# A four-layer graph network: one hand-written order of steps for every engine replaced by another, with a table of banks

## What is computed

```python
def _L0_gnn_ref(x, adj, Wq, bq, Wk, bk, Wv, bv, Wo, bo, gamma, beta):
    ...
    logits = jnp.einsum('bhqd,bhkd->bhqk', q, k) / np.sqrt(DK)
    logits = logits + jnp.log(jnp.clip(adj, ADJ_MIN, None))[:, None, :, :]
    attn = jax.nn.softmax(logits, axis=-1)
    out = jnp.einsum('bhqk,bhkd->bhqd', attn, v)
    out = out.transpose(0, 2, 1, 3).reshape(b, n, d)
    out = out @ Wo.T + bo
    return _layer_norm(x + out, gamma, beta)

def _L1_gnn_ref(feats, adj_mat, fc_w, fc_b, q_w, q_b, k_w, k_b):
    ...
    feat_proj = jnp.einsum('bnh,oh->bno', feats, fc_w) + fc_b
    q = jnp.einsum('bnh,oh->bno', feat_proj, q_w) + q_b
    k = jnp.einsum('bnh,oh->bno', feat_proj, k_w) + k_b
    logits = q + jnp.swapaxes(k, 2, 1)
    masked = logits + (1.0 - adj_mat) * NEG_INF
    masked = jnp.where(masked >= 0, masked, LEAKY_SLOPE * masked)
    atten = jax.nn.softmax(masked, axis=-1)
    out = jnp.einsum('bnm,bmh->bnh', atten, feat_proj)
    return out + feats

def _L2_gnn_ref(x, adjacency, W_q, b_q, W_k, b_k, W_v, b_v, w_g, b_g):
    ...
    scores = jnp.einsum('bihd,bjhd->bhij', Q, K) / jnp.sqrt(jnp.float32(hd))
    soul_bias = a[:, :, None] + c[:, None, :] + b_g
    scores = scores + (soul_bias + jnp.log(adjacency + EPS))[:, None, :, :]
    attn = jax.nn.softmax(scores, axis=-1)
    out = jnp.einsum('bhij,bjhd->bihd', attn, V).reshape(B, N, D)
    return out + x

x = _L0_gnn_ref(x, adj, ...)
x = _L1_gnn_ref(x, adj, ...)
x = _L2_gnn_ref(x, adj, ...)
x = _L3_gnn_ref(x, adj, ...)   # as _L1, with other weights
return x
```

## Time and profile before

| | us |
|---|---|
| median of 3 runs | 1798.22 |
| lowest and highest | 1797.73, 1798.81 |
| span of the profiled execution | 1798.2 |
| PE busy | 1757.7 |
| DVE busy | 1475.6 |
| ACT busy | 1372.0 |
| POOL busy | 731.3 |

### The profile page before, as it was taken

The page is one execution under the profiler, slowest core; times in us unless marked ns, Lnnn a source line. Parts: engine busy times, 40 slices in busy tenths (PEclk is TensorE's granted clock), DMA queues, the critical chain, the costliest instruction groups (busy, mean ns, idle before and its releaser), DMA issues.

```text
span 1798.2 us, 68824 instructions
## 1 busy us (share of the span) xinstructions
PE 1757.7 (98%) x28155; PEld 1647.2 (92%) x28155; DVE 1475.6 (82%) x3361; ACT 1372.0 (76%) x3792; POOL 731.3 (41%) x797
## 2 busy tenths in 40 slices
PE   7999999999999999999999999999999999999997
PEld 6899999999999999999999999999999999999986
DVE  4688888888888888888888888888888888888875
ACT  3677787777787787787787787787787787787774
POOL 3343344343443343443443343343443443443421
PEclk8999999999999999999999999999999999999999
DMA  3101011011011011011011011011011011011100
GB/s 116 39 20 49 26 49 49 26 49 50 26 49 49 26 49 49 27 49 49 26 49 50 26 49 50 26 49 49 26 49 49 26 49 49 26 49 49 35 8 25
DMA packets 48261, 74.56 MB, mean 41 GB/s; under 512 B 5456, under 2 KB 21968, under 8 KB 47952
## 3 DMA queue, kind: packets, MB, share of 16 engines
q1 hardware_dynamic: 47376, 69.49, 12.1%
q10 hardware_dynamic: 576, 0.68, 0.1%
HBM read 53.37 MB, written 16.78 MB: 39 GB/s over the span
## 4 chain that ended last, share of the span: by engine, by line
PE 87%; ACT 3%; DMA 3%; DVE 3%; issue 2%; POOL 2%; SPq 0%; DVEq 0%; POOLq 0%; ACTq 0%
PE banks L1111 15%; PE banks L1176 14%; PE banks L1113 13%; PE banks L1112 13%; PE banks L1325 7%; PE banks L1220 6%; PE banks L1211 6%; DMA x_t<-x_t_dram 3%; PE banks L1199 2%; PE banks L1285 2%; PE banks L1225 2%; PE banks L1313 1%; PE banks L1319 1%; POOL weights_B L684 1%; PE banks L1279 1%
## 5 line engine op out<-in xcount | busy, mean ns | idle before, releaser
L684 POOL TENSOR_TENSOR weights_B<-weights_B,adj 128x512 f32<-128x512 f32 x64 | 113.0, 1766 | 299.1 <-ACT weights_B L765 299.1
L690 POOL TENSOR_TENSOR inv_parts_A<-inv_both_A,own 128x512 fp32r<-128x512 f32 x64 | 66.7, 1042 | 303.7 <-DVE inv_both_A L1035 303.7
L1000 DVE TENSOR_REDUCE least_cols_A<-banks 128x4 f32<-128x512 f32 x256 | 159.4, 684 | 33.8 <-PE banks L1176 33.7
L1000 DVE TENSOR_REDUCE least_B<-banks 128x4 f32<-128x512 f32 x256 | 172.6, 681 | 11.6 <-PE banks L1185 11.5
L1111 PE MATMUL banks<-w_hi_v,xt_hi 128*128 128x258 f32 (+1 forms) x512 | 157.3, 307 | 9.5 <-DVE pick L883 9.5
L1111 PE MATMUL banks<-w_hi_f,xt_hi 128*128 128x258 f32 x512 | 162.3, 317 | 2.3 <-DVE xt_lo L875 0.7
L839 ACT ACTIVATE fp<-banks 128x258 f32<-128x258 f32 x256 | 92.6, 390 | 89.1 <-PE banks L1113 89.1
L765 ACT ACTIVATE banks<-banks,v_B 128x256 f32<-128x256 f32 x384 | 153.4, 474 | 0.0
L1111 PE MATMUL banks<-xt_hi,w_hi_k 128*128 128x256 f32 x512 | 150.7, 294 | 0.3 <-DVE xt_lo L875 0.3
L1113 PE MATMUL banks<-w_lo_v,xt_hi 128*128 128x258 f32 (+1 forms) x512 | 145.1, 283 | 0.0
L1112 PE MATMUL banks<-w_hi_v,xt_lo 128*128 128x258 f32 (+1 forms) x512 | 145.0, 283 | 0.0
(11 more groups left out here) (192 smaller groups left out, 6172.0 us busy)
## 6 DMA issues: line engine op xcount, KB each, us to landing
x_t<-x_t_dram SPq DMA_DIRECT2D x64, 256.0 KB, 3.6
x_in<-x_dram SPq DMA_DIRECT2D x64, 256.0 KB, 3.6
out_dram<-x_out SPq DMA_DIRECT2D x64, 256.0 KB, 2.4
adj_t<-adj_t_dram SPq DMA_DIRECT2D x64, 128.0 KB, 3.4
adj<-adj_dram SPq DMA_DIRECT2D x64, 128.0 KB, 2.0
scratch<-weights_dram SPq DMA_DIRECT2D x9, 256.0 KB, 6.6
...
```

Of the source, the lines that this page charges most:

```text
L684: pool.tensor_tensor(units, units, weight_of[where][:, G.four, :, :].unsqueeze(2).broadcast_to([P, GROUP, 2, P]), ALU.mult).then_inc(first ...
L1000: dve.tensor_reduce(to, bank[SCORE_BANKS[n]].rearrange("p (u m) -> p u m", u=UNITS), axis=AX.X, op=ALU.min).then_inc(maxed[where], 1)
```

## The change

The operations are the same. Every engine gets a new order of the steps of a turn (ORDER), and new lists for the first and last turns (EARLY, LATE; LATE now begins one turn earlier and lists SP's steps too). On PE, q 0 and k 0 open the turn, den B and use B come ahead of scores A, turn_p 3 and mix 3 come earlier, and scores B follows den A and use A. On DVE, den A and mix 3 come ahead of all four max B, and xt_lo of stream 2 behind out_proj. On POOL, bias 0 follows den A, and penalty comes next, ahead of weigh B; turn_x 0 and adj_t come behind den B. The banks 4 to 7 are given by a table (HOMES) in place of the rotation. FILLERS has other places and counts, 164 in place of 143. SP's loop is written in another way and issues the same sequence. EARLY and LATE (some 400 lines of steps in the same notation) are left out below, and ACT's list.

```diff
 ORDER = {
     "tensor": [
-        (0, "k", "0", 0), (1, "out_proj", "0", 0), (1, "out_proj", "0", 1), (0, "q", "0", 0), (2, "v", "2", 0),
-        (2, "k", "2", 0), (0, "scores", "A", 0), (3, "use", "B", 0), (3, "den", "B", 0), (2, "v", "2", 1),
-        (1, "turn_x", "1", 0), (0, "turn_max", "A", 0), (0, "again", "A", 0), (0, "shift", "A", 0), (1, "fc", "1", 0),
-        (3, "wide", "B", 0), (1, "fc", "1", 1), (2, "q", "2", 0), (1, "mask", "1", 0), (2, "turn_rows", "2", 0),
-        (-1, "v", "0", 0), (4, "turn_p", "3", 0), (2, "scores", "B", 0), (0, "den", "A", 0), (0, "use", "A", 0),
-        (4, "mix", "3", 0), (3, "fc", "3", 0), (1, "turn_p", "1", 0), (3, "fc", "3", 1), (0, "wide", "A", 0),
-        (1, "mix", "1", 0), (3, "mask", "3", 0), (2, "turn_max", "B", 0), (2, "again", "B", 0), (2, "shift", "B", 0)],
+        (0, "q", "0", 0), (0, "k", "0", 0), (1, "out_proj", "0", 0), (1, "out_proj", "0", 1), (3, "den", "B", 0),
+        (3, "use", "B", 0), (0, "scores", "A", 0), (2, "v", "2", 0), (2, "k", "2", 0), (1, "turn_x", "1", 0),
+        (2, "v", "2", 1), (0, "turn_max", "A", 0), (0, "again", "A", 0), (0, "shift", "A", 0), (4, "turn_p", "3", 0),
+        (1, "fc", "1", 0), (3, "wide", "B", 0), (2, "turn_rows", "2", 0), (1, "fc", "1", 1), (2, "q", "2", 0),
+        (1, "mask", "1", 0), (-1, "v", "0", 0), (4, "mix", "3", 0), (0, "den", "A", 0), (0, "use", "A", 0),
+        (2, "scores", "B", 0), (3, "fc", "3", 0), (1, "turn_p", "1", 0), (3, "fc", "3", 1), (0, "wide", "A", 0),
+        (1, "mix", "1", 0), (3, "mask", "3", 0), (2, "turn_max", "B", 0), (2, "again", "B", 0),
+        (2, "shift", "B", 0)],
     "vector": [
-        (0, "max", "A", 2), (0, "max", "A", 3), (3, "den", "B", 0), (1, "turn_x", "1", 0), (3, "wide", "B", 0),
-        (3, "sum", "2", 0), (1, "qk", "1", 0), (0, "weigh", "A", 1), (0, "weigh", "A", 2), (1, "mask", "1", 0),
-        (0, "weigh", "A", 3), (1, "leak", "1", 0), (3, "turn_x", "3", 0), (2, "max", "B", 0), (1, "inv", "1", 0),
-        (2, "max", "B", 1), (0, "den", "A", 0), (2, "max", "B", 2), (4, "mix", "3", 0), (2, "max", "B", 3),
-        (3, "qk", "3", 0), (2, "max_parts", "B", 0), (0, "wide", "A", 0), (1, "mix", "1", 0), (3, "mask", "3", 0),
-        (0, "split", "A", 0), (3, "leak", "3", 0), (1, "turn_x", "2", 0), (2, "weigh", "B", 1),
-        (0, "out_proj", "0", 0), (2, "weigh", "B", 2), (2, "weigh", "B", 3), (-1, "adj_t", "", 0),
-        (0, "out_proj", "0", 1), (3, "inv", "3", 0), (0, "norm", "", 0), (-1, "max", "A", 0), (-1, "max", "A", 1)],
+        (3, "den", "B", 0), (1, "turn_x", "1", 0), (3, "wide", "B", 0), (3, "sum", "2", 0), (1, "qk", "1", 0),
+        (0, "weigh", "A", 1), (0, "weigh", "A", 2), (1, "mask", "1", 0), (0, "weigh", "A", 3), (3, "turn_x", "3", 0),
+        (1, "leak", "1", 0), (4, "mix", "3", 0), (0, "den", "A", 0), (1, "inv", "1", 0), (2, "max", "B", 0),
+        (2, "max", "B", 1), (2, "max", "B", 2), (2, "max", "B", 3), (3, "qk", "3", 0), (2, "max_parts", "B", 0),
+        (0, "wide", "A", 0), (3, "mask", "3", 0), (0, "split", "A", 0), (1, "mix", "1", 0), (3, "leak", "3", 0),
+        (2, "weigh", "B", 1), (2, "weigh", "B", 2), (2, "weigh", "B", 3), (0, "out_proj", "0", 0),
+        (0, "out_proj", "0", 1), (1, "turn_x", "2", 0), (-1, "adj_t", "", 0), (3, "inv", "3", 0), (0, "norm", "", 0),
+        (-1, "max", "A", 0), (-1, "max", "A", 1), (-1, "max", "A", 2), (-1, "max", "A", 3)],
     "scalar": [
...
     "gpsimd": [
-        (0, "turn_x", "0", 0), (0, "bias", "0", 0), (4, "den", "B", 0), (4, "bias", "3", 0), (1, "weigh", "A", 0),
-        (1, "den", "A", 0), (3, "weigh", "B", 0), (1, "penalty", "", 0), (1, "rstd", "", 0), (-1, "adj_t", "", 0)],
+        (1, "penalty", "", 0), (3, "weigh", "B", 0), (1, "rstd", "", 0), (3, "den", "B", 0), (-1, "turn_x", "0", 0),
+        (-1, "adj_t", "", 0), (0, "weigh", "A", 0), (3, "bias", "3", 0), (0, "den", "A", 0), (0, "bias", "0", 0)],
     "sync": [
         (-1, "load", "", 0), (4, "store", "", 0)],
 }
...
-BANK = {key: OTHER_BANKS[OTHERS.index(key) % len(OTHER_BANKS)] if key in OTHERS else SCORE_BANKS[0] for key in LAG}
+HOMES = {
+    ("q", "0", 0): 4, ("k", "0", 0): 5, ("out_proj", "0", 0): 6, ("out_proj", "0", 1): 7, ("den", "B", 0): 5,
+    ("use", "B", 0): 4, ("v", "2", 0): 7, ("k", "2", 0): 6, ("turn_x", "1", 0): 4, ("v", "2", 1): 7,
+    ("turn_max", "A", 0): 6, ("turn_p", "3", 0): 5, ("fc", "1", 0): 6, ("wide", "B", 0): 4, ("turn_rows", "2", 0): 5,
+    ("fc", "1", 1): 7, ("q", "2", 0): 6, ("mask", "1", 0): 5, ("v", "0", 0): 7, ("mix", "3", 0): 4,
+    ("den", "A", 0): 6, ("use", "A", 0): 7, ("fc", "3", 0): 7, ("turn_p", "1", 0): 4, ("fc", "3", 1): 6,
+    ("wide", "A", 0): 5, ("mix", "1", 0): 7, ("mask", "3", 0): 6, ("turn_max", "B", 0): 4}
+BANK = {key: HOMES[key] if key in HOMES else SCORE_BANKS[0] for key in LAG}
 
 
 FILLERS = {
-    (("den", "A", 0), 0): 7, (("wide", "A", 0), 0): 11, (("turn_max", "A", 0), 1): 9, (("mask", "1", 0), 0): 4,
-    (("den", "A", 0), 1): 3, (("k", "0", 0), 2): 8, (("mix", "1", 0), 0): 3, (("turn_x", "1", 0), 1): 3,
-    (("turn_p", "1", 0), 1): 3, (("turn_rows", "2", 0), -3): 3, (("out_proj", "0", 0), -1): 3, (("k", "2", 0), -2): 5,
-    (("turn_p", "3", 0), -4): 3, (("v", "2", 0), -1): 5, (("wide", "B", 0), -2): 2, (("mix", "3", 0), -3): 3,
-    (("den", "B", 0), -1): 22, (("wide", "B", 0), -1): 11, (("mix", "3", 0), -2): 3, (("fc", "3", 0), -1): 4,
-    (("mask", "3", 0), -1): 4, (("turn_p", "3", 0), -1): 21, (("mix", "3", 0), -1): 3}
+    (("v", "0", 0), 1): 3, (("wide", "A", 0), 0): 15, (("turn_x", "1", 0), 0): 23, (("mask", "1", 0), 0): 8,
+    (("turn_p", "1", 0), 0): 8, (("mask", "3", 0), -4): 3, (("use", "B", 0), -3): 14, (("fc", "1", 0), -1): 3,
+    (("v", "2", 0), -1): 8, (("den", "B", 0), -2): 3, (("wide", "B", 0), -2): 6, (("den", "B", 0), -1): 30,
+    (("wide", "B", 0), -1): 6, (("turn_p", "3", 0), -1): 30, (("mix", "3", 0), -1): 4}
 
 
...
 
         FIRST_OF_SUMS = min((("den", "A", 0), ("use", "A", 0)), key=lambda step: OTHERS.index(step))
         LATE_BANK = BANK[FIRST_OF_SUMS]
-        PRODUCT_BANK = OTHER_BANKS[(OTHERS.index(("turn_max", "A", 0)) - 1) % len(OTHER_BANKS)]
+        PRODUCT_BANK = BANK[OTHERS[OTHERS.index(("turn_max", "A", 0)) - 1]]
         TOGETHER = product_done["beta", 0]
         fills = Fills(GROUPS)
 
                     sp.dma_start(out[G.no], x_out[:, G.odd, :]).then_inc(stored[G.odd], 16)
 
             load_weight("k0")
-            first, *others = steps("sync")
-            step(first[0], first[3])
-            for n in ("o0", "f1", "k2", "q2", "f1_rows", "f3_rows", "v2", "f3"):
-                load_weight(n)
-            for name, _, _, G in others:
+            for i, (name, _, _, G) in enumerate(steps("sync")):
                 step(name, G)
+                if i == 0:
+                    for n in ("o0", "f1", "k2", "q2", "f1_rows", "f3_rows", "v2", "f3"):
+                        load_weight(n)
             for i in range(2):
```

More of the change, by code:

```diff
@@ new lines @@
+    "vector": [
+        (0, "max", "A", 0), (0, "max", "A", 1), (0, "max", "A", 2), (0, "max", "A", 3), (0, "adj_t", "", 0),
+        (0, "weigh", "A", 1), (0, "weigh", "A", 2), (0, "weigh", "A", 3), (0, "den", "A", 0), (0, "wide", "A", 0),
+        (0, "split", "A", 0), (0, "out_proj", "0", 0), (0, "out_proj", "0", 1), (1, "max", "A", 0),
+        (1, "max", "A", 1), (0, "norm", "", 0), (1, "max", "A", 2), (1, "adj_t", "", 0), (1, "max", "A", 3),
+        (0, "turn_x", "1", 0), (1, "weigh", "A", 1), (0, "qk", "1", 0), (1, "weigh", "A", 2), (0, "mask", "1", 0),
+        (1, "weigh", "A", 3), (0, "leak", "1", 0), (2, "adj_t", "", 0), (1, "den", "A", 0), (0, "inv", "1", 0),
+        (1, "wide", "A", 0), (1, "split", "A", 0), (0, "mix", "1", 0), (1, "out_proj", "0", 0),
+        (0, "turn_x", "2", 0), (1, "out_proj", "0", 1), (2, "max", "A", 0), (1, "norm", "", 0), (2, "max", "A", 1),
[2 rows of a table added]
@@ L107 @@
         (1, "inv", "1", 0), (0, "max", "B", 0), (0, "max", "B", 1), (0, "max", "B", 2), (0, "max", "B", 3),
[2 rows of a table removed]
-        (2, "out_proj", "0", 1), (0, "weigh", "B", 3), (2, "norm", "", 0), (3, "max", "A", 0), (3, "max", "A", 1),
[1 row of a table removed]
+        (0, "max_parts", "B", 0), (2, "wide", "A", 0), (3, "adj_t", "", 0), (1, "mix", "1", 0), (2, "split", "A", 0),
+        (1, "turn_x", "2", 0), (0, "weigh", "B", 1), (0, "weigh", "B", 2), (0, "weigh", "B", 3),
+        (2, "out_proj", "0", 0), (2, "out_proj", "0", 1), (0, "den", "B", 0), (2, "norm", "", 0), (3, "max", "A", 0),
[1 row of a table added]
@@ L112 @@
         (0, "sum", "2", 0), (2, "qk", "1", 0), (3, "weigh", "A", 1), (3, "weigh", "A", 2), (2, "mask", "1", 0),
[3 rows of a table removed]
-        (0, "leak", "3", 0), (4, "adj_t", "", 0), (2, "turn_x", "2", 0), (1, "weigh", "B", 1),
-        (3, "out_proj", "0", 0), (3, "out_proj", "0", 1), (1, "weigh", "B", 2), (1, "weigh", "B", 3),
```

(32 more changed lines are left out.)

37 lines of the change are left out of this document (12 added, 25 removed), and 312 rows, old and new, of tables (EARLY, LATE, ORDER).

## The result

| | before | after |
|---|---|---|
| median of 4 runs, us | 1797.97 | 1824.95 |
| lowest and highest | 1795.31, 1798.81 | 1823.96, 1827.44 |
| span of the profiled execution | 1798.2 | 1822.2 |
| PE busy | 1757.7 | 1778.3 |
| DVE busy | 1475.6 | 1539.3 |

The changed kernel takes 1.0158 times as long (95% interval 1.0144 to 1.0173): 27 us more, where 32 were forecast. The two spans are only 24 us apart, because the profiled execution after was the fastest of its four (1823.96 us, 1.8 above its span), and the one before, whose span is as long as the median time, was by the same 1.8 a slower one.

What follows compares the result with a forecast made beforehand. PE, busy 98% of the span, was taken to bound the kernel. From 1798.2 us, loads -7.3, DVE-POOL collisions at max_parts +42.8 and first and last turns -3 gave 1830.7, say 1830 us, range 1796 to 1850.

Steps and rivals of the forecast that it cites:

- What bounds the kernel: PE, busy 98% of the span, sets the time; every new wait of PE is paid in each of 57 turns.
- The loads: SP's adj and x_t go out earlier once POOL's penalty leaves its place behind weigh B, removing 7.3 us of waits.
- The collision at max_parts: POOL's bias0 and penalty hold up DVE's qk3, top and least_cols; PE's turn_max B 0.75 us late a turn, 42.8 us.
- the walk: Step times added from old rows, from den A's start on PE: qk3 due at 5.83, turn_max B at 6.99, not 6.27.
- my lower bound: At max_parts, qk3 and top slip in and only least_cols waits for the penalty's second half: 0.43 us a turn.
- qk1 under weigh A: DVE's qk1 falls under POOL's weigh A and shifts the reciprocal and POOL's chain later; 0.35 us taken for the upper bound.
- PE's own steps: Same matmuls, about as many shape changes between neighbours: counted as nothing, with 0.1 us a turn (6 us) either way.
- First and last turns: Outside 200 to 1700 us, a few waits gained against some collisions: -3 us, between -9 and +3.
- The sum: Whole kernel: 1798.2 - 7.3 + 42.8 - 3 = 1830.7, say 1830 us.
- The faster one: Rival: POOL's chain doesn't meet max_parts, nothing is blocked and only gains remain: 1785 us, chance 0.18.
- The far slower one: Rival: POOL keeps the lock from one operation to the next, a turn loses 1.8 us: 1891 us, chance 0.02.
- No change: Rival: collisions of 0.1 to 0.2 us a turn, 6 to 11 us, eat the gains: 1798 us, chance 0.05.

Runs made afterwards that it cites:

- load_late_again: The changed kernel with POOL's penalty back behind weigh B (groups 6 to 60), bias0 keeping its new place: 1805.58 us, ratio 1.0046 to the kernel before.
- pen_early: The changed kernel with POOL's penalty moved ahead of den A in the turns of groups 6 to 60: 1798.46 us, ratio 1.0006 to the kernel before.
- pen_bias: The changed kernel with POOL's penalty ahead of den A and bias3 ahead of weigh A, groups 6 to 60: 1792.85 us, ratio 0.9981 to the kernel before.
- pen_bias_tail: pen_bias with penalty(61) moved likewise and POOL's list of the last turns reordered by the same rule: 1790.39 us, ratio 0.9964 to the kernel before.
- old_with_new_place: The kernel before with only POOL's bias0 and penalty moved between den A and weigh B, groups 7 to 60: 1809.95 us, ratio 1.0076.

## Why the prediction was right, and where its sizes were off

*What bounds the kernel* held: PE sets the time, and the loss comes as stands of PE ahead of turn_max B: 0.48 us later in the median turn, of which the list of waits shows 0.3 and the rest counts as busy.

*The loads* (-7.3 us): right. Their waits are gone, and load_late_again, which brings them back, costs 7.1 us. Weigh B, clear of xt_lo, takes 1.30 us as forecast (at 907.00), where it took 1.82.

*The collision at max_parts* (+0.75 us a turn, between 0.43 and 1.07): the mechanism is the one predicted, down to the operations and the ends. The size was too large by half of what was measured, 0.50 by pen_early. The step that failed is where qk3 falls: I had it due inside the penalty's second half, with all three behind that. Measured from the start of den A (897.30 in the turn shown), qk3 starts at 5.80, as the walk had it (5.83), but POOL's rows lie 0.3 later: bias0 at 4.15 and not 3.81, the halves at 5.39 and 6.09 and not 5.09 and 5.79. That carried qk3 under the first half, from which it and top got away together, and only least_cols waited for the second. That is the case of my lower bound (0.43), whose terms were off in both directions: the second half ends 0.3 later than in the walk, and least_cols ends 0.03 after it and not its full 0.17, as the row of top in the earlier trace rows had already shown (85.93 against 85.90). I had taken lateness on POOL only to add to the stall, and it also changed which operations are caught; what the stall would be without it no run shows.

*qk1 under weigh A*: predicted as something that shifts the chain, not as a cost of its own. It does both: freeing it takes 0.08 us off the turn, and brings POOL's inv_parts A from 3.17 to 2.91 us behind den A in the median turn (pen_early and pen_bias).

*PE's own steps* (0, with 0.1 either way): pen_bias, free of both collisions, has 26.85 us against 26.80 in an undisturbed turn of before, so 0.05. The list of waits shows none for a bank in the repeated turn.

*First and last turns* (-3 us): -5.5 + 2.6 = -2.9, right as a sum, though I had no parts for it, and by luck: up to 2.6 us of the first part are the clock's time of return, which differs between executions of the same first turns. The last turns lose 2.6 us. Part of it is POOL's operations on DVE's, shown by pen_bias_tail (1.2 us from scores A of group 63 on). The rest is argued only. PE stands ahead of mix 3 of group 62, which shares bank 4 with wide B of group 63, until DVE has read that bank; the granted clock is at 0.63 in the stretch after, where the trace before has 1.00 in all of its last turns:

```profile
1807.25 1.81 PE L1364 MATMUL banks<-fpt,fp 128*128 128x128 f32 x8 [1.59 <-DVE sum_t L1087]
```

```profile
1808.00:1812.00 4.00, 3.56 (x17) 3.15 (x16) 0.86 (x1) 0.77 (x2) 0.31 (x1) 0.63 0.00 0
```

Another bank for that one step wasn't tried. The waits of PE that the profile lists from scores A of group 63 on add up to 7.0 us, and to 8.1 before, so they alone don't make the difference; and in old_with_new_place, which has the old lists, the clock falls in the last turns too (0.72 granted from 1784 to 1788 us), and they take 84.8 us.

*The sum*: 57 turns at 27.43 and not 26.98, with a few turns of other length, make the 26.9 us; predicted were 42.8 - 7.3 = 35.5. These 8.6 us are the whole distance of 1830.7 from the span of 1822.2, since the first and last turns came out as forecast, by luck. From the median of 1824.95 the forecast of 1830 is 5 us off.

*The rivals.* The faster one (1785, POOL's chain doesn't meet max_parts) is what pen_bias makes true by design: 1793 there, 1790 with the last turns mended. I had put it too low mainly by counting 3 us of gain on PE's own steps, which cost 0.05 us a turn (2.9 us). The far slower one (POOL keeps the port from one operation to the next) falls in the rows above: at 921.89 and 903.31 the waiting DVE operation got in ahead of POOL's next. "No change" is nearest to pen_early (1.0006), where 0.08 us a turn of collision and 0.05 of PE's own, 7.4 us in 57 turns, eat the loads' gain.
